# Two adaptive-layernorm transformer blocks on one core: normalisations on ScalarE, new instruction orders, and a setup split up among the first pairs

## The reference

```python
x = L0_attn_X
mod = (_silu(L0_c) @ L0_wmod).reshape(L0_c.shape[0], 6, 1, -1)
...
ga = (2 * (ga >= 0) - 1) * jnp.maximum(jnp.abs(ga), 0.25)
h = _layernorm(x, axis=-1) * (1 + ca) + sa
x = x + ga * _L0_attn_ref(h, ...)      # one head of 128, softmax over 256 keys
h = _layernorm(x, axis=-1) * (1 + cb) + sb
x = x + gb * _L0_ffn_ref(h, ...)       # 352 hidden, both operands rounded to FP4 in blocks of 16
...                                    # the same modulation from L1_c, L1_wmod
x = x + ga * _L1_attn_ref(h, ...)      # 16 heads of 8, causal
h = _layernorm(x, axis=-1) * (1 + cb) + sb
x = x + gb * _L1_ffn_ref(h, ...)       # 4 live experts of 704 hidden, the best 2 weighted
```

## Time and profile before

| | us |
|---|---|
| median of 3 runs | 1906.21 |
| lowest to highest of them | 1902.27 to 1909.68 |
| the profiled execution's own time | 1907.06 |
| its span | 1905.3 |

### The profile page before, as it was taken

The page is one execution under the profiler, slowest core; times in us unless marked ns, Lnnn a source line. Parts: engine busy times, 40 slices in busy tenths (PEclk is TensorE's granted clock), DMA queues, the critical chain, the costliest instruction groups (busy, mean ns, idle before and its releaser), DMA issues.

```text
span 1905.3 us, 37018 instructions
## 1 busy us (share of the span) xinstructions
PE 1699.7 (89%) x12297; PEld 1317.1 (69%) x12297; DVE 1678.0 (88%) x3791; ACT 716.5 (38%) x1447; POOL 68.9 (4%) x78
## 2 busy tenths in 40 slices
PE   2347799999999999999999999999999999999998
PEld 1234567776776767677686767777676777768787
DVE  5578799989899998989989998999989899997775
ACT  0122435262533426253432526243352525334332
POOL 0000000000000000000000000000000000000000
PEclk7686899999999999999999999999999999999999
DMA  4020302003030301203030110303021030303000
GB/s 142 25 76 28 109 5 89 28 20 98 5 107 10 104 14 27 86 15 97 10 105 13 50 63 18 99 5 106 12 63 51 18 99 6 100 10 91 12 13 8
DMA packets 130106, 97.25 MB, mean 51 GB/s; under 512 B 28000, under 2 KB 124512, under 8 KB 125824
## 3 DMA queue, kind: packets, MB, share of 16 engines
q1 hardware_dynamic: 121536, 91.74, 16.4%
q10 hardware_dynamic: 8448, 4.20, 0.7%
HBM read 56.48 MB, written 29.98 MB: 45 GB/s over the span
## 4 chain that ended last, share of the span: by engine, by line
PE 47%; DVE 37%; issue 9%; ACT 4%; SPq 1%; DVEq 1%; DMA 1%; POOL 0%; ACTq 0%; POOLq 0%
DVE mneg L1099 9%; PE y_ps L1476 9%; PE bank L1469 5%; PE bank L1471 5%; PE bank L1470 5%; DVE h L1196 4%; PE bank L1220 4%; DVE tt L1188 3%; PE bank L1436 3%; ACT arena L770 2%; DVE xh L967 2%; PE bank L1343 2%; DVE arena L1107 2%; PE bank L1373 2%; PE bank L1420 2%
## 5 line engine op out<-in xcount | busy, mean ns | idle before, releaser
L813 ACT ACTIVATE tt<-bank 128x512 f32<-128x512 f32 x352 | 212.4, 603 | 665.8 <-PE bank L1471 523.9
L1476 PEld LDWEIGHTS y_ps<-wd,h 128*128 128x128 f32 (+1 forms) x3072 | 379.1, 192 | 70.7 <-issue 19.1
L1476 PE MATMUL y_ps<-wd,h 128*128 128x128 f32 (+1 forms) x3072 | 415.4, 282 | 14.1 <-DVE h L1196 14.1
L1196 DVE TENSOR_TENSOR h<-tt,bank 128x512 f32<-128x512 f32 x352 | 236.0, 682 | 23.6 <-PE bank L1471 7.1
L1188 DVE SCALAR_TENSOR_TENSOR tt<-tt,bank 128x512 f32<-128x512 f32 x352 | 237.2, 682 | 21.4 <-ACT tt L813 14.7
L1099 DVE TENSOR_REDUCE mneg<-bank 128x2 f32<-128x512 f32 (+1 forms) x384 | 236.0, 680 | 3.9 <-issue 2.4
L770 ACT ACTIVATE arena<-bank 128x512 f32<-128x512 f32 x384 | 196.5, 612 | 34.8 <-PE bank L1417 20.7
L1469 PE MATMUL bank<-h_hi,wg_hi 128*128 128x512 f32 x352 | 164.2, 466 | 10.3 <-DVE h_lo L1163 3.8
L1469 PE MATMUL bank<-h_hi,wu_hi 128*128 128x512 f32 x352 | 163.1, 463 | 8.4 <-DVE mneg L1099 8.3
L1107 DVE TENSOR_TENSOR arena<-arena,keep_k 128x1024 f32<-128x1024 f32 (+1 forms) x96 | 149.0, 1577 | 20.4 <-ACT arena L770 18.8
L1471 PE MATMUL bank<-h_lo,wg_hi 128*128 128x512 f32 x352 | 140.5, 399 | 0.0
(11 more groups left out here) (183 smaller groups left out, 2647.0 us busy)
## 6 DMA issues: line engine op xcount, KB each, us to landing
q_stack<-q_rows SPq DMA_DIRECT2D x16, 1024.0 KB, 4.8
k_stack<-k_rows SPq DMA_DIRECT2D x16, 1024.0 KB, 8.0
q_rows<-qk_halves SPq DMA_DIRECT2D x48, 256.0 KB, 2.8
k_rows<-qk_halves SPq DMA_DIRECT2D x48, 256.0 KB, 2.9
rows<-mod_rows SPq DMA_DIRECT2D x48, 128.0 KB, 3.0
rows<-mod_rows SPq DMA_DIRECT2D x16, 384.0 KB, 3.5
x_in<-in_L_attn_X SPq DMA_DIRECT2D x16, 256.0 KB, 2.8
vals<-arena SPq DMA_DIRECT2D x128, 32.0 KB, 5.2
```

What stands on the lines that cost most here:

```text
L813: send(a(tt[:, ch % 2, :], ps.bank(f"eg{ch}")[:], ACT.Tanh, scale=0.5), tanh_ready)
L1196: frees(v.tensor_tensor(h32[:, ch % 3], tt[:, ch % 2, :], ps.bank(f"eu{ch}")[:], ALU.mult), f"eu{ch}")
L1476: ins = mm(y_ps[:, P * t:P * (t + 1)], h32[rows_, ch % 3, P * t:P * (t + 1)], wd[rows_, ch, :], start=first and t == 0, stop=last_ and t = ...
```

## The change

Three things are changed.

1. The four normalisations of a pair are applied by ScalarE, as `rstd * x + shift`. GpSimd makes the shift, -mean x rstd, in a second instruction behind the power; VectorE makes -mean in one instruction more in `stats`.
2. All order tables and the banks' table are new, from the same kind of planner with larger assumed margins from the end of an engine's instruction to the start of one that waits for it.
3. The setup is split up. The conditioning vectors and their matrices have a semaphore of their own. The 31 weight transfers are issued by ScalarE, which also makes the upper halves. The FP4 rounding, its transposes and the lower halves are hung behind steps of the first pair (`follow`). The clamps are merged. x_in is loaded before the modulation rows are stored.

```diff
-SMALL = 15
+SMALL = 11
...
 def dve_order(do):
-    do(1, "maxima", 5), do(0, "begin"), do(0, "times", 6), do(0, "mix", 0), do(1, "turn_max"), do(2, "quantise_h", 0, 1)
...
+    do(2, "quantise_h", 0, 1), do(1, "turn_max"), do(0, "times", 6), do(2, "gate0", 2), do(2, "gate0", 3), do(0, "begin")
...
+        def turns(eng, order, mine, follow={}):
...
+                        it = Turn(reg, plus + lead)
+                        mine[name](it, *which)
+                        if first_pair(it) and (name, *which) in follow:
+                            follow[(name, *which)]()
...
         @block.sync
             def load1(it):
                 sp.wait_ge(x1_ready.sem, x1_ready.before(it, 1))
                 send(sp.dma_start(x_in[:], x_v[bass.ds(it.scaled(1), 1)].rearrange("o t k d -> (o t) k d")), x_loaded)
+                if first_pair(it):
+                    sp.wait_ge(s_rows_ready, 1)
+                    sp.dma_start(mod_rows, row_tile).then_inc(s_rows, 16)
+                    sp.wait_ge(s_rows, 16)
                 send(sp.dma_start(rows1[:], rows_from(it, 0, 1)), rows1_loaded)
...
         @block.gpsimd
-            def root(it, n, var, rstd, k):
+            def root(it, n, var, rooted, rstd, k):
                 pool.wait_ge(var.sem, var.at(it, k))
-                send(g.tensor_tensor(n.rstd[:], n.ve[:], mhalf[:], ALU.pow), rstd)
+                send(g.tensor_tensor(n.rstd[:], n.ve[:], mhalf[:], ALU.pow), rooted)
+                pool.wait_ge(rooted.sem, rooted.at(it, k))
+                send(g.tensor_tensor(n.shift[:], n.mv[:, :, 0], n.rstd[:], ALU.mult), rstd)
...
         @block.scalar
-            act.wait_ge(s_ld, 16 * SMALL)
-            a(res[0:NB, 0:2, :], x_in[0:NB, 0:2, :], ACT.Tanh, scale=0.5).then_inc(s_act0, 1)
+            act.wait_ge(s_cond, 16 * 4)
+            a(res[0:NB, 0:2, :], mixed[0:NB, 0:2, :], ACT.Tanh, scale=0.5).then_inc(s_act0, 1)
             act.wait_ge(s_ct, 1)
             a(sct, y_ps[:, 0:2 * NB], ACT.Copy).then_inc(s_sct, 1)
...
+            act.wait_ge(s_zero, 1)
+            for n, w in enumerate((w_gate, w_up)):
+                for c, (c_at, c_n) in enumerate(FCH):
+                    act.dma_start(fp4_in[0:c_n, 3 * n + c, :], w[c_at:c_at + c_n, :]).then_inc(s_fp4, 16)
...
+            act.wait_ge(s_w[0], 16 * 8)
+            a(wg_hi[:], stage[0], ACT.Copy).then_inc(s_split, 1)
+            act.wait_ge(s_w[1], 16 * 8)
+            a(wu_hi[:], stage[1], ACT.Copy).then_inc(s_split, 1)
+            act.wait_ge(s_ld, 16 * SMALL)
...
+            def normalise(it, n, k, src, dst, rstd, done):
+                act.wait_ge(rstd.sem, rstd.at(it, k))
+                for t in range(TILES):
+                    last = a(dst[:, t, :], src[:, t, :], ACT.Identity, scale=n.rstd[:, t:t + 1], bias=n.shift[:, t:t + 1])
+                send(last, done)
...
+                            halves4=halves4, gate=gate, finish=finish), {("scores0", 1): fp4_gate, ("probs0", 1): fp4_up, ("turn2",): fp4_down_})
...
         @block.vector
-            for j in (2, 5, 8, 11):
-                clamp(modt[:, j, :], modt[:, j, :], res[:, 0, 0:NB], res[:, 1, 0:NB])
+            gates = modt[:, 2:12:3, :]
+            clamp(gates, gates, *[res[:, n, 0:4 * NB].rearrange("p (j b) -> p j b", b=NB) for n in range(2)])
...
             def stats(it, step, n, src, var):
...
                 step(last)
+                v.tensor_scalar(n.mv[:, :, 0], n.mv[:, :, 0], -1.0, None, ALU.mult)
                 send(v.tensor_scalar(n.ve[:], n.mv[:, :, 1], EPS, None, ALU.add), var)
...
+            def lower_halves():
+                dve.wait_ge(s_split, 2)
+                v.tensor_tensor(wg_lo[:], stage[0], wg_hi[:].bitcast(F32), ALU.subtract).then_inc(s_ready, 1)
+                v.tensor_tensor(wu_lo[:], stage[1], wu_hi[:].bitcast(F32), ALU.subtract).then_inc(s_ready, 1)
...
+                            finish=finish), {("stats1",): fp4_halves, ("quantise_x", 2): fp4_third, ("value0",): lower_halves})
...
         @block.tensor
+            def fp4_turn(n):
+                pe.wait_ge(s_fp4q, n + 1)
...
+                           finish=finish), {("scores0", 1): lambda: fp4_turn(0), ("out0",): lambda: fp4_turn(1), ("turn2",): lambda: fp4_turn(2)})
```

More of the change, by code:

```diff
@@ L430, in send, with first_pair @@
             ins.then_inc(s.sem, s.step)
-        def turns(eng, order, mine):
+        def first_pair(it):
+            return it.reg is None and it.plus == 0
+        def turns(eng, order, mine, follow={}):
             def turn(reg, plus):
@@ L961, in stats @@
                 step(last)
+                v.tensor_scalar(n.mv[:, :, 0], n.mv[:, :, 0], -1.0, None, ALU.mult)
                 send(v.tensor_scalar(n.ve[:], n.mv[:, :, 1], EPS, None, ALU.add), var)
-            def normalise(it, n, k, src, dst, rstd, done):
-                own(it, rstd, k)
-                for t in range(TILES):
-                    last = v.tensor_scalar(dst[:, t, :], src[:, t, :], n.mv[:, t, 0:1], n.rstd[:, t:t + 1], ALU.subtract, ALU.mult)
-                send(last, done)
             def stats1(it):
@@ L1505, in finish @@
                 down(it, CHUNKS - 1)
+            def fp4_turn(n):
+                pe.wait_ge(s_fp4q, n + 1)
+                if n:
+                    pe.wait_ge(s_fp4c, n)
+                for c, (c_at, c_n) in enumerate(FCH):
+                    if n < 2:
+                        last = turn(y_ps[:, c_at:c_at + c_n], fp4_in[0:c_n, 3 * n + c, :], c_n)
+                    else:
+                        last = turn(y_ps[0:c_n, P * c:P * (c + 1)], fp4_down[:, c_at:c_at + c_n])
+                last.then_inc(s_fp4t, 1)
             turns(pe, pe_order, dict(turn1=turn1, query0=query0, key0=key0, value0=value0, scores0=scores0, probs0=probs0, out0=out0,
```

286 lines of the change are left out of this document (140 added, 146 removed), and 47 rows, old and new, of the table USES.

## The result

The changed kernel takes 1861.75 us, the median of 4 runs (1855.89 to 1863.49); the kernel before took 1906.99 beside it. The ratio is 0.9762, with a 95% interval of 0.9746 to 0.9779. It is faster by 45 us where the prediction said 69: inside the range of 1808 to 1884, but 24 us over the predicted 1838, and 4 us outside the forecast's own range.

What follows compares the result with a forecast made beforehand. TensorE and VectorE were taken to wait for each other by turns, VectorE the heavier. Gains of 20 (setup), 5 (filling), 42 (turns) and 2 (drain) made 69 off 1907, so 1838 us; own range 1820 to 1858, wider 1808 to 1884.

Steps and rivals of the forecast that it cites:

- rival 1: Loop: TensorE's waits stay, VectorE's freed time becomes its own waits, turn falls 1 us or less; 1872 to 1882; chance 0.18.
- Setup: Start to first gate product of layer 0: it comes at about 72 instead of 91.98; 20 us gained, bounds 14 and 24.
- Filling: Pipeline fill to 317 us: VectorE loses nine normalisations but the chain lengthens; 5 us gained, bounds 9 gained and 3 lost.
- Loop turns: Twelve full turns: each 3.5 us shorter, at 106.3, with 2.5 us of waits left; 42 us gained, bounds 12 and 64.
- Drain: End of the run, bound by TensorE with its work unchanged: 2 us gained, bounds 6 gained and 2 lost.
- Rival 4: Loop: normalisations in ScalarE's in-order queue hold the gates, 2 us at each of four places; slower, 1936; chance 0.07.
- Rival 3: Setup does not pay: ScalarE's blocked queue and inserted FP4 work cut its gain to 5 us; 1858; chance 0.07.
- three things that I named as showing it wrong: Turn over 108.8 us, VectorE or TensorE waiting for a tanh behind a normalisation, or first gate product later than 78 us.

Runs made afterwards that it cites:

- b_setup: The kernel before with the new split-up setup alone, its orders and VectorE normalisations kept; 1904.03 us.
- b_setup_actnorm: The kernel before with the new setup and the normalisations moved to ScalarE, in the orders of before; 1874.92 us.
- a_dvenorm: The changed kernel with the normalisations back on VectorE, new orders and setup kept; 1920.03 us.
- a_late: The changed kernel with ScalarE's two casts moved behind the first normalisation and eight w2 transfers issued by SyncE; 1850.22 us.
- A_swish_straight: The changed kernel with its loop written out and VectorE's product with gate 17's tanh moved ahead of the next pair's block scales; 1826.71 us.
- a_straight: The changed kernel with its eleven loop turns written out, same instructions and order; 1873.11 us.
- a_late_straight: The changed kernel with two casts behind the first normalisation, the w2 transfers on SyncE and its loop turns written out; 1869.07 us.
- B_straight: The kernel before with its loop turns written out; 1894.98 us.

## Why the prediction was right, and where it was 24 us off

The kind of gain was foreseen, its size less well: three of the four pieces gave less than forecast and the last one more, and the time lies in the stated range only by the part of it that rival 1 had opened above 1858.

**Setup: 16.3 us, not 20.** The early tanh was mis-sized by little (6.13; I had 3 us earlier than 9.92), the rows' work took 7.1 us as reckoned. ScalarE was late as the prediction said, but by 3 us more: its 31 transfers took 20.0 us to issue, where SyncE's rows had 16.2, so it ended at 27.9 instead of 25.6; the casts cost what was reckoned, and the four activations 1.64 instead of 1.2. In b_setup, where the normalisation does not queue behind the casts, the second load comes at 52.7 instead of 59.2.

**Filling: 1.4 lost, not 5 gained, by the fifth load.** This step failed. The prediction gave 5 us for VectorE's relief in a stretch that it itself called bound by latency, and priced the new orders there at nothing. The runs show the price in two parts, by the fifth load: 27.0 us gained with the setup alone, 22.6 with ScalarE's normalisations in the old orders, 14.9 in the new. The new orders are worst between the second and the third load: 61.7 us against 52.9 in b_setup_actnorm, and with the normalisations on VectorE 61.5 in a_dvenorm against 52.8 in b_setup. That they are made for a full turn, and put steps of one pair between steps that the other needs next, is a likely reason, but was not traced.

**Loop turns: 1.9 us, not 3.5.** The mechanism held. VectorE was relieved by 3.6 us (I had 3.7 to 4.3), its 98.7 us a turn is the forecast 98.5, and TensorE became the engine whose own work sets the turn. The sum that gave 106.3 was 103.8 us of TensorE's work and 2.5 of waits left; measured are 103.4 and 4.5. So the term that was mis-sized is the waits: 2.0 us too few, and 1.6 of that is the issue row at the branch, a pause that the kernel before has on VectorE (2.4 us in ten turns) but not on TensorE, and that the prediction has no term for. The rest of the waits, 2.9, was nearly right. The work hides a second miss. The prediction took the loop's clock of 1.00 as given. By the rows above a fall costs 1.5 us, so seven falls are about 10 of the 1034 us, and without them TensorE's work is 102.4 a turn, 1.4 less than I had; the two misses nearly cancel, which is luck. Six of the seven falls stand right behind the pause at the branch, where TensorE's first work is now the transposes that need a bank freed by one of the last maxima, and one behind the fourth normalisation. Pause and falls together, some 26 us in ten turns, are more than the 16 that are missing, since the work without falls was 14 us less than forecast.

That the branch makes the pause is shown by the four written-out kernels, in which the issue rows are gone. Why one pause is followed by a fall and the next one not is open: in the changed kernel three of the nine turns with the pause have no fall, and the kernel before has TensorE busy 1.30 of 2 us in a turn without one and 1.34 in a turn with one.

**Drain: 12.3 with the last turn's share, not 5.5.** The new orders drain better than I gave them: the setup alone leaves 380.4 us from the last load to the end as before, and ScalarE's normalisations in the old orders 383.8, but a_dvenorm has 376.2 and the changed kernel 368.1. Some 3 us of the 12.3 are the clock's, an estimate from 10.3 us at half clock there before and 3.4 now. It was luck that this piece gave 6.8 us more than forecast: without it the time would have been about 1869, nearer the end of the range, 1884, than its middle.

**ScalarE.** The trace has 485 ns for an activation whose scale and bias are read from tiles; the 293 ns of the earlier trace rows is a plain copy and was the wrong neighbour. The Trainium skill, ScalarE: Activation LUTs (Rules for kernel authors), which the prediction weighed and put behind the row, was right: its 6.5 us a turn stands beside the measured 6.7. It did not matter for the bound, since ScalarE is busy 51 of 108 us.

**The rivals.** Rival 1 (waits stay) gave 1872 to 1882; the result lies between it and the forecast. It was right in part: about half of VectorE's freed 3.6 us did turn into its own idle time (7.5 to 9.2 us a turn), but the waits of TensorE that stayed are mostly a new one. Rival 4 (ScalarE's queue holds the gates) was priced at 2 us at each of four places. TensorE's waits for ScalarE's normalisations are 7.3 us in ten turns, 0.7 a turn, and the 1.1 at the product of gate 17 comes from VectorE's order. Rival 3's sum, 1858, is near the time, but by accident: the setup did pay. None of the three things that I named as showing it wrong came true: the turn is 107.9, the first gate product is at 75.73, and VectorE waits for a tanh only 1.7 us in ten turns.

**The branch.** The issue idle before an engine's first work of a loop turn is up to 0.4 us in the kernel before, 1.9 in b_setup and 2.3 in the changed kernel. The Trainium skill, Runtime: NRT & Kernel Launch (Instruction fetch mechanics), says that a taken branch whose target has left the instruction window waits for a fetch; the issue rows, which go when the loop is written out, agree. By its advice to unroll, the changed kernel should have gained; it lost 11 us: TensorE's idle time fell from 4.5 to 2.5 us a turn, but 102 us at half clock instead of 24 cost more. Why the same loop body pays 0.4 in one kernel and 1.9 in another, and why a_late's pauses are fewer, stays open: the position of the code and what the transfers do at that moment both differ, and neither was tried alone.

## What to carry to other kernels

Read the granted clock in short stretches along the loop, not as a mean: 0.99 instead of 1.00 hid 24 us at half speed in ten turns, and each fall of 3.4 us cost 1.5 us of TensorE's time. A sum of work and waits needs both the pauses at a loop's branch and these falls as terms of their own. Two small waits of TensorE side by side can cost more than their sum; where a wait can't be removed, moving it away from the next one may be enough, as it was here. When one part of a change seems worth nothing, look at a mark ahead of the loop and at one behind it: b_setup was 28 us ahead and gave it back, and only those two marks show it.

## What the runs showed of the hardware

- Falls of the clock come behind short pauses of an otherwise full TensorE: 0.45 busy of 2 us, or 1.5 and 0.73 of two such stretches in a row. Such a pause does not always bring one: the changed kernel has pauses of 1.70 us without a fall and of 1.74 us with one, and the kernel before 1.30 busy of 2 us without and 1.34 with. A_swish_straight has 1.36, 1.97, 1.63 and 1.47 in a row without a fall. What else decides is open.
- Small pauses can be enough: in b_setup_actnorm falls stand behind a microsecond with TensorE busy 0.68 or 0.69 between full ones.
- Falls can lock to the turn: in a_straight ten turns of 109.1 to 109.5 us each had one of about 10 us; a_late_straight had turns of 105.1, 105.0, 106.4 and 104.7, and then seven of 109.3. One program thus has two paces within one execution, 4 us a turn apart. B_straight, in the orders of before, has them too: 107.7 us in the first turns and 109.2, with 6.8 us at half clock, in four later ones.
- A change outside the loop moved the loop's time: the setup alone by +2.0 us a turn, and the casts moved behind the first normalisation give five turns near 105.2 instead of one.
